# Up products issued ahead of a step's waits for PSUM banks, and up weights of the second layer's experts streamed from DRAM

## The reference, cut to what matters

```python
x = x + L0_xattn(ctx, layernorm(x), mask)          # 8 heads, 77 keys
x = x + L0_ffn(layernorm(x))                       # 8 experts of 704, each row goes to 2
x = x + L1_xattn(layernorm(x), ctx, ...)           # rows @ W_in.T + a scanned patch term
x = x + L1_ffn(layernorm(x))                       # 32 experts of 128, each row goes to 6

# L0_ffn: sum over a row's 2 experts of p * ((silu(x @ Wg) * (x @ Wu)) @ Wd), plus a shared expert
# L1_ffn: sum over a row's 6 experts of w * (relu(x @ up_e.T) ** 2 @ down_e.T), plus a shared expert
```

## Time and profile before

| what | number |
|---|---|
| median of three runs | 836.36 us |
| the profiled execution | 839.08 us, its span 837.3 us |
| PE, busy share of the span | 87% |
| DVE, ACT, POOL | 50%, 33%, 37% |
| mean granted TensorE clock | 0.953 of full |
| DMA moved | 179.58 MB, mean 214 GB/s |
| chain that ended last | PE 46%, POOL 18%, DVE 16%, issue 12% |
| L587, up of the first layer | 189.8 us busy, 26.7 us idle before |
| L779, up of the second layer | 64.6 us busy, 13.5 us idle before |
| L1722, DVE's copies of up weights | 114 of them, median 286 ns |

### The profile page before, as it was taken

How to read it: one execution, slowest core, us unless ns; L and a number is a source line. 1 busy time by engine, 2 the same in 40 slices (tenths; PEclk the granted TensorE clock), 3 DMA queues, 4 the chain that set the end, 5 groups by cost and what they waited for, 6 DMA issues and landing times.

```text
span 837.3 us, 14551 instructions
## 1 busy us (share of the span) xinstructions
PE 732.2 (87%) x4718; PEld 638.7 (76%) x4718; DVE 422.7 (50%) x1633; ACT 277.4 (33%) x608; POOL 309.8 (37%) x328
## 2 busy tenths in 40 slices
PE   3989998999999999888789888969796999998865
PEld 3777787899999998778778877746564787886754
DVE  5998868323332424342754267156420455567653
ACT  2644532221111111223122312123432566666530
POOL 1332321750011101000112443561775477777650
PEclk9996887999999999999999999989999999999998
DMA  8999991339667668535744662542576766698966
GB/s 259 393 292 266 262 265 34 109 105 329 228 217 241 218 207 282 165 124 157 249 155 146 223 229 92 181 163 82 183 264 209 225 224 213 217 321 279 314 217 241
DMA packets 93242, 179.58 MB, mean 214 GB/s; under 512 B 9825, under 2 KB 54966, under 8 KB 93022
## 3 DMA queue, kind: packets, MB, share of 16 engines
q1 hardware_dynamic: 77760, 137.05, 52.7%
q0 software_dynamic: 13344, 38.68, 12.2%
q10 hardware_dynamic: 2046, 2.71, 1.1%
HBM read 132.45 MB, written 65.62 MB: 237 GB/s over the span
## 4 chain that ended last, share of the span: by engine, by line
PE 46%; POOL 18%; DVE 16%; issue 12%; DMA 4%; ACT 2%; SPq 1%; DVEq 0%; POOLq 0%; ACTq 0%
PE PB L587 19%; PE PB L618 10%; POOL rows_out L1866 9%; POOL rows_in L1830 5%; POOL sorted_x L1812 4%; PE PB L779 2%; PE PB L505 2%; DMA X<-in_x 2%; PE PB L644 1%; PE PB L788 1%; DVE BNS L1085 1%; PE PB L602 1%; ACT MEM L919 1%; DVE WK L1214 1%; PE PB L819 1%
## 5 line engine op out<-in xcount | busy, mean ns | idle before, releaser
L587 PE MATMUL PB<-XT,MEM 128*128 128x128 f32 x1584 | 189.8, 279 | 26.7 <-ACT XT L894 19.2
L587 PEld LDWEIGHTS PB<-XT,MEM 128*128 128x128 f32 x1584 | 183.8, 194 | 31.2 <-issue 30.6
L1821 POOL DMA_INDIRECT sorted_y<-WK x36 | 34.5, 958 | 282.4 <-DVE WK L1443 282.4
L1830 POOL DMA_INDIRECT rows_in<-MEM x96 | 94.3, 982 | 49.3 <-issue 28.8
L618 PE MATMUL PB<-MEM,WK 128*128 x432 | 99.2, 379 | 0.0
L618 PEld LDWEIGHTS PB<-MEM,WK 128*128 128x128 f32 x432 | 79.3, 190 | 9.3
L779 PE MATMUL PB<-MEM,WK 128*128 128x128 f32 x456 | 64.6, 286 | 13.5 <-DVE WK L1722 11.8
L779 PEld LDWEIGHTS PB<-MEM,WK 128*128 128x128 f32 x456 | 56.3, 194 | 21.4 <-issue 14.0
L1866 POOL DMA_INDIRECT rows_out<-WS,MEM x58 | 56.9, 981 | 33.7 <-ACT WS L1006 20.3
L894 ACT ACTIVATE XT<-PB 128x256 f32<-128x256 f32 x52 | 19.8, 381 | 144.8 <-PE PB L564 144.8
L788 PE MATMUL PB<-MEM,WK 128*128 x228 | 62.6, 399 | 3.4 <-issue 2.8
(11 more groups left out here) (277 smaller groups left out, 1240.1 us busy)
## 6 DMA issues: line engine op xcount, KB each, us to landing
MEM<-in_w SPq DMA_DIRECT2D x36, 896.0 KB, 7.1
rows_in<-in_consts SPq DMA_DIRECT2D x32, 600.0 KB, 11.8
MEM<-in_w SPq DMA_DIRECT2D x36, 512.0 KB, 4.0
MEM<-rows_in SPq DMA_DIRECT2D x58, 300.0 KB, 4.1
MEM<-rows_out SPq DMA_DIRECT2D x16, 768.0 KB, 7.8
MEM<-in_w SPq DMA_DIRECT2D x32, 256.0 KB, 3.3
MEM<-in_w SPq DMA_DIRECT2D x2, 3072.0 KB, 19.4
sorted_x<-MEM SPq DMA_DIRECT2D x1, 5070.0 KB, 39.2
```

Of the source, the lines that this page charges most:

```text
L587: t = e.matmul(o[:, to:to + P], UPW[m][i % (3 - m)][:, k, c * P:(c + 1) * P], XT[:, n % 2, k, :], start=(k == 0), stop=(k == 1))
L1821: e.indirect_dma_start(out=DY, out_offset=bass.IndirectOffsetOnAxis(ap=DEST[:, i:i + 1], axis=0), in_=YS[:, i % 2, :], in_offset=None).the ...
L1830: e.indirect_dma_start(out=DX1, out_offset=bass.IndirectOffsetOnAxis(ap=SLOT1[:, i, j:j + 1], axis=0), in_=XR[:, i, :], in_offset=None).th ...
```

## The change

Two edits. In the first, `up` no longer waits ahead of its products: a step's PE work comes after the whole of up0, by a new function `between`, which waits only for the bank that the step uses. ACT does the gates first and then all of a step's work. In the second, W1E keeps only the 256 columns of down weights (the loads in `after_blocks` are 128 KB), and SP brings the up weights of a pair from DRAM to W1U, four buffers, two transfers of 128 KB a pair, three pairs ahead; the first three pairs are issued before the first fetch of rows. DVE's copies and the buffer WUP are gone. PE's up2 waits for the transfer. PE now waits for the expert table and the W1E loads itself.

```diff
-        W1E = MEM[:, 0:E1 * 512].rearrange("p (e c) -> p e c", e=E1)
+        W1E = MEM[:, 0:E1 * 256].rearrange("p (e c) -> p e c", e=E1)
+        W1U = MEM[:, 9216:11264].rearrange("p (a b c) -> p a b c", a=4, b=2)
...
             def up(n, nb):
                 kind, i = item(n, nb)
-                steps = list(steps_of(n, nb))
-                if steps:
-                    q.wait_ge("y", n - 2)
-                    if n + 1 < EARLY + nb + LATE:
-                        q.wait_ge("xtb", n + 1)
...
-                            if c == 3 and m == 0:
-                                for g, k in steps:
-                                    mid(g, k)
                         t.then_inc(*q.mark(f"up{m}", n))
+                        if m == 0:
+                            between(n, nb)
...
-                    for g, k in steps:
-                        mid(g, k)
+                    between(n, nb)
+
+            def between(n, nb):
+                for g, k in steps_of(n, nb):
+                    if k in (1, 2, 4, 5) and n + 1 < EARLY + nb + LATE:
+                        q.wait_ge("xtb", n + 1)
+                    if k in (2, 3, 4, 7):
+                        q.wait_ge("y", n - 2)
+                    mid(g, k)
...
             def up2(s):
                 q.wait_ge("bxt", s)
-                q.wait_ge("bw", s)
+                q.wait_ge(f"wu{s % 4}", s)
...
-                        t = e.matmul(PB[:, 4 + s % 4, j * P:(j + 1) * P], WUP[:, s % 2, j, k * P:(k + 1) * P],
+                        t = e.matmul(PB[:, 4 + s % 4, j * P:(j + 1) * P], W1U[:, s % 4, j, k * P:(k + 1) * P],
...
                 if n < count:                                    # ACT's block_iteration
-                    steps = steps_of(n, nb)
-                    for g, k in steps:
-                        mid(g, k, False)
                     gates(n, nb)
-                    for g, k in steps:
-                        mid(g, k, True)
+                    for late in (False, True):
+                        for g, k in steps_of(n, nb):
+                            mid(g, k, late)
...
-            def weights2(s):                                     # DVE, with its calls and four_experts
-                q.wait_ge("bu", s - 2)
-                for j in range(2):
-                    t = e.tensor_copy(WUP[:, s % 2, j, :], W1E[:, bass.ds(expert(packed, 2 * s + j), 1), 0:256].rearrange(
-                        "p e c -> p (e c)"))
-                t.then_inc(*q.mark("bw", s))
...
-                    e.dma_start(W1E[:, k, :], w1[SC + k]).then_inc(*q.land(f"w1{k // 8}", k))
+                    e.dma_start(W1E[:, k, :], w1[SC + k, :, 256:512]).then_inc(*q.land(f"w1{k // 8}", k))
...
+            def weights2(s):                                     # SP
+                q.wait_ge("tabe")
+                if s // 2 not in packed:
+                    packed[s // 2] = four_experts(q, s // 2)
+                q.wait_ge("bu", s - 4)
+                for j in range(2):
+                    e.dma_start(W1U[:, s % 4, j, :],
+                                w1[bass.ds(expert(packed, 2 * s + j) + SC, 1), :, 0:256].rearrange("e p c -> p (e c)")
+                                ).then_inc(*q.land(f"wu{s % 4}", *((s,) if j else (s, "first"))))
+
+            for s in range(3):
+                weights2(s)
             fetched = 6
             for s in range(6):
                 fetch1(s)

             def step(s, n_pairs, fetched):
+                if 3 <= s + 3 < n_pairs:
+                    weights2(s + 3)
                 for k in range(fetched, min(s + 8, n_pairs + n_pairs % 2)):
                     fetch1(k)
```

More of the change, by code:

```diff
@@ L96 @@
     "cleared": ("set", "hb0"),
+    "rows0_or_up0": ("ga0", "wu0"),
+    "rows1_or_up1": ("ga1", "wu1"),
+    "rows2_or_up2": ("ga2", "wu2"),
+    "rows3_or_up3": ("ga3", "wu3"),
 }.items() for signal in list_}
@@ L392, in build @@
         HT1 = WK[:, 2348:3116].rearrange("p (a b c) -> p a b c", a=3, b=2)
-        WUP = WK[:, 3116:4140].rearrange("p (a b c) -> p a b c", a=2, b=2)
         D2 = WK[:, 3628:3628 + P]
@@ L786, in down2 @@
                 for j in range(2):
-                    w = W1E[:, bass.ds(expert(packed, 2 * s + j), 1), 256:512].rearrange("p e c -> p (e c)")
+                    w = W1E[:, bass.ds(expert(packed, 2 * s + j), 1), :].rearrange("p e c -> p (e c)")
                     t = e.matmul(PB[:, 2 + s % 2, j * D:(j + 1) * D], HT1[:, s % 3, j, :], w, start=True, stop=True)
@@ L1695, in dve_program @@
             number1 = e.value_load(PAGES, min_val=0, max_val=P)
-            packed = {}
             def meta1(k):
@@ L1744, in step @@
                 if s + 1 < n_pairs and (s + 1) % 2 == 0:
[L1745 to L1751, removed]
                     meta1((s + 1) // 2)
@@ L1756, in step @@
                     e.tensor_tensor(ht, ht, PB[:, 4 + s % 4, 0:256], ALU.mult).then_inc(*q.mark("bh", s))
-                if 0 < s + 1 < n_pairs:
-                    weights2(s + 1)
                 if s in SUM6:
@@ L2016, in store @@
                 e.dma_start(od[:, i:i + 2, :], X[:, i:i + 2, :]).then_inc(*q.land("out_a", i))
+            packed = {}
+            def weights2(s):
+                q.wait_ge("tabe")
+                if s // 2 not in packed:
[7 more added lines that the diff above has]
+                weights2(s)
             fetched = 6
@@ L2038, in end1 @@
                 n_pairs, k = PAIRS[c], fetched
+                packed.clear()
                 for s in range(COMMON, n_pairs + 2):
```

## The result

The changed kernel takes 808.11 us (median of 4 runs, 807.0 to 814.23) against 836.26 us for the kernel before (4 runs, 835.99 to 838.14): ratio 0.9674, 95% interval 0.9623 to 0.9725. The profiled execution took 807.0 us for a span of 805.2, before 837.3, so 32.1 us went.

| stretch of PE | before | after | difference |
|---|---|---|---|
| start to the last shared product (L755, after L760) | 640.38 | 609.53 | -30.85 |
| from there to the first up product of the second layer (L779, after L784) | 10.12 | 14.01 | +3.9 |
| its 56 steps, to the last up product | 154.87 | 149.83 | -5.0 |
| from there to the end | 31.9 | 31.8 | -0.1 |

What follows compares the result with a forecast made beforehand. First-layer blocks bound by PE, second layer by PE and POOL equally. The first edit gains 27.2 us, the second nothing; 27 off the 836.36 median gives 809.2, said as 810, own range 803 to 817, 8 in 10 802 to 827.

Steps and rivals of the forecast that it cites:

- Part 1: First-layer routed blocks: removing 16 bank waits ahead of up products, less waits that come back, gains 27.2 us.
- the thin cover of step 0: First group's step 0: without waits up0 would end at 340.8, 0.3 us behind XT's being ready at 340.5.
- The two waits that were to come: New PE waits: 3.5 us ahead of L630 in the second group, about 1.3 us at the first late shared block.
- Part 2, the start: Second layer's start: six weight issues ahead of the first row fetch make PE start 2 us later (1 to 4).
- Part 2, "a PE step without a wait still takes 2.57 us": Second layer's 56 steps would take 144 us against 154.9, so removing weight-copy waits gains at most 9 us.
- Part 2, late weights: Second layer while routed rows return: DMA overloaded, up products wait for late weights in two clusters, 7 us in sum.
- R4: Every second-layer weight transfer lands late, over 10.3 us, with SP issuing everything in one order: slower, 845 us; chance 0.04.
- POOL's scatters beside copies: Second layer: removing DVE's weight copies takes at most 4 us of work off POOL; not used in the sum.
- R1: DMA becomes the second layer's bound, share near 1, steps 2.8 us from the first: 826 us; chance 0.20.
- the estimate of 5 us: Over 731 to 757, streaming would need 431 GB/s against a 358 GB/s HBM limit: a 5 us stretch, near the 6.
- R2: First layer: DVE and ACT take the place of the bank waits, halving that gain to 14: 822 us; chance 0.13.
- R3: Both edits pay: second-layer weights are never late, 7 us more gained: 802 us; chance 0.11.

Runs made afterwards that it cites:

- e8: Changed kernel with one of the three first pairs' weights issued behind the first two row fetches; 935.59 us, ratio 0.9678 to the kernel before.
- e1: First edit alone on the kernel before, up weights still copied by DVE; 942.8 us, ratio 0.9767 to the kernel before.
- e3: First edit without streaming, DVE copying the next pair's up weights ahead of the current pair's multiply; 927.26 us, ratio 0.960 to the kernel before.
- e4: Changed kernel with the first eight fetches of finished rows and all their sums two steps later; 937.77 us, ratio 0.9706 to the kernel before.
- e6: Second run, on another chip, of the changed kernel with eight finished-row fetches and all sums two steps later; 938.6 us, ratio 0.9693 to the kernel before.
- e9: Changed kernel with the first eight fetches of finished rows two steps earlier; 936.17 us, ratio 0.9737 to the kernel before.

## Why the prediction was right, and where it was not

It said 810, 802 to 827; the time is 808.11. The mechanism of the first part holds. In the second part the length of PE's step and the issues at the start were wrong; that the part still came out near nothing is luck.

- *Part 1, 27.2 us.* 30.85 in the first profiles. The waits that were to go went, the thin cover of step 0 held, steps 1 to 5 hid the move of the step's work. The two waits that were to come are 2.85 and 0.94 us, not 3.5 and 1.3: 1.0 of the 3.65 us missing. Another 2.9 lie in the routed block where the engines have just taken their branch by the number of blocks: 44 entries of the up product at 484.96 took 6.80 us behind 1.51 of "issue" in the kernel before, and 5.17 behind 0.27 now, an entry that I left out of the sum.

```profile
484.96 6.80 PE L587 MATMUL PB<-XT,MEM 128*128 128x128 f32 x44 [1.51 <-issue]
```
```profile
460.82 5.17 PE L586 MATMUL PB<-XT,MEM 128*128 128x128 f32 x44 [0.27 <-issue]
```

- *Part 2, the start, 2 us (1 to 4).* 3.9. The spare time was there: SP's wait of 2.8 us for the last scattered rows is gone. The issues were mis-sized: the six took 4.67 us, 0.8 each, not 3.0, and the second turn waits 0.65 us more for its rows. e8 puts a price of 2 us on each pair's weights.
- *Part 2, "a PE step without a wait still takes 2.57 us", at most 9 us to gain.* Wrong. PE's step is 2.20 us; 2.57 was the ring through DVE, as e1 and e3 show. I took "no named wait" for "bound by PE", though the weight load's row at 672.20 has 0.33 us of "issue" just ahead of it. The floor of 144 us for 56 steps is about right all the same, for POOL and not for PE: at 2.53 us per pair, which stood in my text, its train can't take less than 143.1 us, and PE ahead of it gains nothing. PE gained 12.7 us from pair 0 to 34 (77.2 us, before 89.8); POOL's whole train is 4.4 us shorter than before.
- *Part 2, late weights, 7 us in two clusters.* The waits come to 17.7 us in 8 places; the clusters stand where they were expected. Of these, PE could bear what it was ahead of POOL: PE lost 7.6 us against the kernel before over pairs 34 to 56, POOL's train has some 9 us of gaps. A single place, the 5.93 us at pair 35, I had not seen: SP itself waited at the fetch, with the DMA engines at a share of 0.41. The text had SP's order only in R4. What share of the other waits (11.8 us in 7) comes from the order and what from full DMA engines is open: e4, e6 and e9 did not settle it. Landings of the weights of 9.2 and 9.6 us, against the 7.9 us that I had worked out for four buffers, would make some by themselves.
- *POOL's scatters beside copies, up to 4 us, kept out of the sum.* Nothing came of it: the 114 scatters take 112.9 us together, before 112.6. The reading of the 1.03 us scatter was loose too. The two copies ran from 718.86 to 719.35 and the scatter began at 719.15, so 0.2 us of copying lay beside it, not 0.5, and it took a third of that longer, not a seventh.
- *No rival in the main.* R1's condition, DMA share near 1 through the whole stage, did come true (0.98, 1.03, 1.00), and yet the steps went at 2.20 us: with share 0.98 in the quiet part PE waited for DMA once between pair 3 and pair 34, 0.53 us. A share of 1 was not the bound that R1 took it for; the engines moved 333 GB/s there and 377 later. The Trainium skill (DMA: Bandwidth & Descriptors, Where 436 GB/s comes from) gives about 358 GB/s as a core's HBM limit, and the same page says right ahead of it that this is a core's part when both cores of a pair stream. One core ran here, and 377 over 25 us is above the figure, so the estimate of 5 us that I had set beside mine from it has no ground in this trace, and the measurement decides. R2 failed: L623 and L635 wait once each. R3 needed the weights in time; e3 gets that by not streaming. R4 failed: the weights' landings stayed under 10.3 us.

In the profiled executions the kernel gained 32.1 us: 3.65 more than forecast in the first part and 1.1 in the second (-5.0 + 3.9) in place of nothing. The medians differ by 28.2, since the profiled execution of before lies 2.8 us above its median and that of after 1.1 below; this, too, brings the time near 810.

## What to carry to other kernels

A step that repeats with the same length and no named wait is not thereby at its engine's floor: add up the ring through the other engines, and look for an instruction in it that could be issued one place earlier before paying for it with traffic. When an engine gets faster, see which one it runs ahead of, and which in-order queue then stands at a wait for that one with somebody else's data behind it. A wait moved behind work that does not need it is worth its idle time plus the draining, and can be priced well from the block beside it that has none.

## What was not expected of the hardware

The same kernel takes 836 us in its first runs and 965 to 969 on the three chips of the experiments. The blocks without a step are alike (5.08 us for 44 entries of the up product in both, and e1), though their code is passed through once like all the rest; behind them the chain of e1 stands still for up to 27.59 us at "another core or an unknown queue". Experts' steps that are 2.20 us in the first profile of the changed kernel are 2.2 to 7.7 us on these chips. What it is that they wait for, the profile does not name, and the cause stays open.

DMA engines that are busy all the time can still move more. In the changed kernel's first profile the engines are busy for 90% or more of every half microsecond from 680 to 700, but the last, and from 740 to 760. What they moved there:

```profile
DMA packets 5705, 7.17 MB, mean 358 GB/s; under 512 B 686, under 2 KB 5184, under 8 KB 5703
```
```profile
DMA packets 4702, 7.89 MB, mean 395 GB/s; under 512 B 562, under 2 KB 3878, under 8 KB 4700
```

The second stretch moved fewer but larger packets: the busy share alone does not tell how much more fits.
